# Cross-attention stack on one core: where TensorE's side steps stand between scores and outputs

## The reference, cut to what matters

```python
q = split_heads(x @ wq); k = split_heads(ctx @ wk); v = split_heads(ctx @ wv)
attn = softmax(q @ k.T * scale)      # 56 queries a head, 1500 keys (1496 in the third piece)
x = (attn @ v) joined @ wo + bo + x  # 20 heads of 64, 8 heads of 20, 20 heads of 8
```

## Time and profile before

| what | value |
|---|---|
| median of 3 runs | 5894.31 us (5889.82 to 5895.18) |
| the profiled execution, its own time | 5887.77 us |
| its span | 5886.0 us |
| TensorE busy (matmul) | 5530.6 us, 94% |
| TensorE weight loads | 4544.8 us, 77% |
| VectorE / ScalarE / GpSimd busy | 2818.9 / 3097.9 / 3117.4 us (48 / 53 / 53%) |
| mean granted clock of TensorE | 0.971 |
| chain that ended last, by engine | TensorE 62%, VectorE 20%, ScalarE 7%, GpSimd 3%, DMA 3%, issue 3% |

### The profile page before, as it was taken

One profiled execution on the slowest core, in us unless ns is written; L12 is line 12 of the kernel. 1 busy time (PEld: TensorE's weight loads), 2 busy tenths in 40 slices (PEclk: granted clock), 3 DMA queues, 4 the chain that ended last, 5 costly groups with the idle time before them and its releaser, 6 DMA issues.

```text
span 5886.0 us, 92283 instructions
## 1 busy us (share of the span) xinstructions
PE 5530.6 (94%) x34224; PEld 4544.8 (77%) x34224; DVE 2818.9 (48%) x5171; ACT 3097.9 (53%) x7280; POOL 3117.4 (53%) x3472
## 2 busy tenths in 40 slices
PE   7999999999999999998999999899999999999998
PEld 5777777778877777776767677578888888888887
DVE  2444454444444444443555555255454555445452
ACT  1455554555555555553555555265666565666655
POOL 0355554454444545553666666166666666566665
PEclk8899999999999999997999999599999999999998
DMA  2000000000000000000111111000000000000000
GB/s 57 13 17 14 17 17 17 17 17 13 14 13 17 17 17 17 14 22 17 31 30 30 32 28 43 11 20 19 17 21 17 21 20 21 17 18 20 17 21 12
DMA packets 85964, 119.97 MB, mean 20 GB/s; under 512 B 42814, under 2 KB 65194, under 8 KB 85514
## 3 DMA queue, kind: packets, MB, share of 16 engines
q1 hardware_dynamic: 85514, 114.07, 6.9%
HBM read 109.56 MB, written 4.46 MB: 19 GB/s over the span
## 4 chain that ended last, share of the span: by engine, by line
PE 62%; DVE 20%; ACT 7%; POOL 3%; DMA 3%; issue 3%; SPq 1%; ACTq 0%; POOLq 0%; DVEq 0%
PE ps_c L701 14%; DVE mpiece L1466 9%; PE ps_s L1141 5%; PE ps_s L1143 5%; PE ps_s L1142 5%; PE ps_c L1084 4%; PE ps_u L1156 4%; PE ps_u L1158 4%; PE ps_u L1157 4%; PE ps_c L1102 3%; POOL p_lo L1622 2%; DVE ctx_hi L1457 2%; DVE uT L1493 2%; ACT p_hi L1835 2%; ACT p L1833 2%
## 5 line engine op out<-in xcount | busy, mean ns | idle before, releaser
L1622 POOL TENSOR_TENSOR p_lo<-p,p_hi 125x448 fp32r<-125x448 f32 (+2 forms) x2688 | 2729.4, 1024 | 2215.3 <-ACT p_hi L1835 1623.4
L1833 ACT ACTIVATE p<-ps_s 125x448 f32<-125x448 f32 (+2 forms) x2688 | 1325.7, 493 | 1882.8 <-PE ps_s L1143 1668.7
L1835 ACT ACTIVATE p_hi<-ps_s 125x448 fp32r<-125x448 f32 (+2 forms) x2688 | 1316.9, 490 | 0.0
L1466 DVE TENSOR_REDUCE mpiece<-ps_c 125x1 f32<-125x500 f32 (+1 forms) x1984 | 1229.3, 668 | 86.0 <-PE ps_c L1084 80.4
L1141 PE MATMUL ps_s<-q_hi,ctxT_hi 105*125 105x448 f32 (+3 forms) x2688 | 999.1, 372 | 35.5 <-ACT p_hi L1835 29.1
L1156 PE MATMUL ps_u<-p_hi,ctx_hi 125*97 125x448 f32 (+2 forms) x2688 | 955.3, 355 | 1.5 <-POOL p_lo L1622 1.0
L1084 PE MATMUL ps_c<-ctxT_hi,q_hi 96*125 96x500 f32 (+1 forms) x2112 | 846.6, 425 | 104.6 <-DVE mpiece L1466 85.3
L1142 PE MATMUL ps_s<-q_lo,ctxT_hi 96*125 96x448 f32 (+2 forms) x2688 | 918.4, 342 | 0.0
L1143 PE MATMUL ps_s<-q_hi,ctxT_lo 96*125 96x448 f32 (+2 forms) x2688 | 916.6, 341 | 0.0
L1157 PE MATMUL ps_u<-p_hi,ctx_lo 125*96 125x448 f32 (+2 forms) x2688 | 909.5, 338 | 0.0
L1158 PE MATMUL ps_u<-p_lo,ctx_hi 125*97 125x448 f32 (+2 forms) x2688 | 909.0, 338 | 0.0
(11 more groups left out here) (228 smaller groups left out, 5861.6 us busy)
## 6 DMA issues: line engine op xcount, KB each, us to landing
ctx_raw<-in_ctx SPq DMA_DIRECT2D x96, 562.5 KB
pT<-recs SPq DMA_DIRECT2D x32, 490.0 KB, 3.6
w_area<-recs SPq DMA_DIRECT2D x32, 490.0 KB, 3.7
w_area<-recs SPq DMA_DIRECT2D x32, 196.0 KB, 3.8
cs<-in_ctx SPq DMA_DIRECT2D x192, 6.0 KB, 2.9
x_between<-x_out SPq DMA_DIRECT2D x32, 80.0 KB
x_in<-x_between SPq DMA_DIRECT2D x32, 80.0 KB
w_area<-in_L_xattn_wq SPq DMA_DIRECT2D x2, 800.0 KB, 5.9
```

The source lines that it names most:

```text
L1466: z = V.tensor_reduce(mpiece[0:wide, k, r:r + 1], C(0, wide, n % banks(t), 0, PIECE), AX.X, ALU.max)
L1622: P.tensor_tensor(p_lo[0:kp, k % 3, 0:w], p32[0:kp, k % 2, 0:w], p_hi[0:kp, k % RING, 0:w].bitcast(F32), ALU.subtract).then_inc(*sig("pl_r ...
L1833: A(p32[0:kp, k % 2, 0:w], ps_s[0:kp, k % 2, 0:w], ACT.Exp, scale=DH[t.ph] ** -0.5)
L1835: A(p_hi[0:kp, k % RING, 0:w], ps_s[0:kp, k % 2, 0:w], ACT.Exp, scale=DH[t.ph] ** -0.5)\
```

## The change

One line of TensorE's `main` goes:

```diff
@@ -1165,7 +1165,6 @@
                         pe.wait_ge(*got("ctx_lo", t, NLO * (b + 1)))
                     if n < total:
                         scores(n)
-                    yield 2 * n + 1
                     if n >= BEHIND or not first:
                         outputs(n - BEHIND)
```

## The result

The changed kernel takes 6053.18 us in the median of 4 runs (6049.38 to 6059.19), the kernel before 5894.75 us (5889.82 to 5896.51) in as many: a ratio of 1.0271, 95% interval 1.0253 to 1.0289. It is slower by 158 us. The forecast had the sign and a third of the size (50 us), and its range ended at 6005 us.

The account below looks back on a forecast made before the run. TensorE's own instruction stream plus its waits was taken to bound the kernel. Losses of 82 us (105 with `maxima` terms halved) less 30 us gains gave +52, said as +50: 5944 us, range 5866 to 6005 us.

Parts of the forecast that it names:

- `pre` 25 to 27: `pre` 25 feeds 27 through two VectorE passes; with 25 behind its outputs, 0.62 us more wait each: 9.3 us loss.
- `pre` 35 to 37: `pre` 35 feeds 37 through VectorE's copy with 0.15 us to spare; a wait of 0.47 us is left: 7 us loss.
- `pre` 2, 4, 16 and the step behind it: Cover gained at some of these steps and lost at others: `pre` 16 net 2 us loss, 2 and 4 taken as nothing.
- context, exponentials, scores: Phases 0 and 2: later context pieces delay ScalarE's copies, exponentials and the scores by 0.62 us, 30 times: 19 us loss.
- phase 1, `pre` 16: A later context piece makes ScalarE later with `xT`, for which `pre` 16 already waits: 15 x 0.65 = 10 us loss.
- outputs that wait themselves, and small ones: Phase 1's first outputs come earlier and wait for a copy, 6.5 us; other outputs and small losses, 5 us.
- gains at `pre` 8 and 34, and in phase 2: Outputs fill waits of `pre` 8 for VectorE and 34 for ScalarE, 9 us gain; a like phase 2 step, 3 us.
- `maxima`, losses halved, less their gains: Losses of 21, 15 and 10 us in phases 1, 2 and 0, halved; gains of 8 us in phase 1, 4 in phase 0.
- Four such places a pair: Phase 1 `maxima` on two banks: three matmuls in a row, the third waiting for VectorE's reductions: 21 us loss.
- counted at every matmul that has less to spare than it loses: Phase 2 `maxima` on three banks, VectorE reducing without pause: 9 us counted once a pair, 37 at every such matmul; 15 taken.
- The rival "much slower": Full `maxima` losses in phases 1 and 2, wider context delays, nothing relieved: +123 us, 6017 us; chance 0.18.
- The switch between kinds of work: 112 blocks of other work than `maxima` between scores and outputs each lose one TensorE switch: 6 us gain taken, 8 at most.

Follow-up runs that it names:

- short reductions: VectorE's maximum taken over only 125 of the 500 columns, in the kernel before and in the changed kernel: 5727.23 and 5773.31 us.
- the mirror of the change: Kernel before with side steps only between the scores and the outputs of a step, none ahead of the scores: 6012.76 us, ratio 1.0218.
- the fastest kernel: Kernel before with sixteen waiting side steps held back, plus a third place ahead of the outputs' last matmul for phase-0 `maxima` only: 5806.07 us, ratio 0.9859.

## Why the prediction was right in sign and wrong in size

Each term of the sum, against what the matched waits show in the changed kernel (us):

| term | forecast | measured |
|---|---|---|
| `pre` 25 to 27 | 9.3 | 8.6 |
| `pre` 35 to 37 | 7 | 6.6 |
| `pre` 2, 4, 16 and the step behind it | 2 | 3 (-3.9, +2.4, -4.1, +8.6 at `pre` 18) |
| context, exponentials, scores | 19 | 22.6 |
| phase 1, `pre` 16 | 10 | 9.8 |
| outputs that wait themselves, and small ones | 6.5 + 5 | 9.2 |
| gains at `pre` 8 and 34, and in phase 2 | -12 | -11.7 |
| not seen: `pre` 1 and context 3 in phase 1 | 0 | -19.9 |
| `maxima`, losses halved, less their gains | 23 - 12 = 11 | 110.4 |
| low clock | 0 | 29 |

**The chains were right.** The rows predicted one by one are there. Timeline of the changed kernel, the same steps of the same pairs as in the earlier trace rows:

```profile
1092.09 2.40 PEld L701 LDWEIGHTS ps_c<-w_area,hT 80*64 80x64 f32 x14 [1.11 <-DVE sm L1232]
...
1106.31 2.44 PE L907 MATMUL ps_c<-pT,kvb 128*128 128x64 f32 x20 [0.31 <-ACT pT L1707]
...
1113.81 0.29 PEld L913 LDWEIGHTS ps_c<-w_s,ones 1*128 1x128 f32 x2 [0.70 <-DVE qo L1331]
...
1619.73 0.18 PEld L1141 LDWEIGHTS ps_s<-q_hi,ctxT_hi 105*125 105x125 f32 x1 [0.81 <-ACT p_hi L1834]
...
3157.35 0.16 PEld L1156 LDWEIGHTS ps_u<-p_hi,ctx_hi 125*97 125x97 f32 x1 [0.93 <-issue]
...
3188.98 0.44 PEld L701 LDWEIGHTS ps_u<-xT,w_s 80*80 80x80 f32 x4 [1.19 <-ACT xT L1722]
```

Line 701 stands idle 1.11 us (1.1 forecast), line 913 0.70 (0.8), the scores behind the context pieces 0.81 where they had 0.19, which is the 0.62 of the outputs, and phase 1's `pre` 16 1.19 where it had 0.73. `pre` 34 waits 0.31 us less. The first outputs of a sequence in phase 1 now start late (row 3157.35); the view names no releaser there, but ScalarE's copy `uT` (line 1822) ends at 3157.24, just ahead.

**The step that failed is the term of the `maxima`:** 11 us net forecast, 110.4 measured. It failed in four places.
- "In phase 0 VectorE is the limit in most of each `maxima` stretch. There only the later start counts: 10 us." The later start did cost about that (8 us, seen where the `maxima` kept their places), but the whole came to 35.5. VectorE was not the limit without a break, as its wait for TensorE in phase 0 shows, before and after. And where it was the limit, its slower conversions (10.7 us more in phase 0) came on top, a term that the forecast did not have.

```profile
DVE mpiece L1466 <- PE ps_c L1084: 15.4, 42, 1.4
```

```profile
DVE mpiece L1465 <- PE ps_c L1084: 49.0, 80, 1.8
```

- "Four such places a pair, on average 0.35: 21 us." This is phase 1, and it came to 34.2, with the gains there already taken off.
- "counted at every matmul that has less to spare than it loses, 37. I take 15, nearer the low one, since after one wait the next ones are covered." This is phase 2. Measured 40.7. A wait does not cover the next ones: in the block it is followed by others, and VectorE catches up while scores and outputs run, so the next block begins from the same state.
- "The terms of `maxima` (21 + 15 + 10) fall where TensorE waits already, and a wait put ahead of these shortens them. I halve these terms". Nothing of the kind shows. The upper count of phase 2, 37, was nearly right, the 21 of phase 1 was too small even unhalved, and phase 0 should have had a count like that of phase 2. The gains that I set against them (8 and 4) are already in the measured sums.

The rival "much slower" named the mechanism in so many words, that joined matmuls leave VectorE idle while scores and outputs follow each other. What I held against it, that three banks hold 1.8 us of its work, is true only of three banks that are all unread. At 848.54 all three hold results, but VectorE is already in the first of them: 1.37 us of work are left, to 849.91, and the next result comes 1.66 us later, at 850.20. Even this rival ended at 6017 us, 36 below what was measured.

The signs that the prediction gave of itself told the same: it expected the wait of line 1084's loads to grow from 221 to some 240 us, most of it in phase 1, and it grew to 326.4, by 34, 30 and 42 us in phases 0, 1 and 2. VectorE's busy time, which should have stayed, grew by 47 us, 31 of them the conversions.

**What had no term at all is TensorE's clock**, the subject of the last section.

## What to carry to other kernels

Where a producer and a consumer exchange a few buffers, count the hand-overs by how they are grouped and not by their average rate: two places a step with one or two matmuls each kept VectorE better fed than one place with up to three, with the `maxima` moved alone, with short reductions and in the mirror of the change. And look at what else the engines do at that moment: an instruction of the consumer can grow from 0.34 to 1.25 us because it now starts behind one of a third engine. Price such a term at every hand-over that has less to spare than it loses, and don't halve it for waits that are there already. And a side step that waits is best held back by itself: a list of sixteen such steps, found in the trace, gave 68 us, while the rule that moved all of them at once lost 158.

## What the runs showed of the hardware that was not expected

**The clock falls more often in the changed kernel.** Three windows of 8 us in the changed kernel, phase 0: busy time of PE, PEld, DVE, ACT and POOL with instruction counts, granted clock, DMA share, GB/s.

```profile
640.00:648.00 8.00, 7.54 (x49) 6.19 (x47) 5.65 (x10) 4.77 (x14) 4.64 (x6) 1.00 0.01 2
648.00:656.00 8.00, 6.84 (x27) 5.31 (x26) 6.00 (x11) 2.42 (x7) 5.14 (x8) 0.79 0.05 12
656.00:664.00 8.00, 7.84 (x37) 5.55 (x35) 7.59 (x14) 3.64 (x10) 3.96 (x5) 1.00 0.23 75
```

TensorE's timeline in the middle one:

```profile
649.28 1.08 PE L1084 MATMUL ps_c<-ctxT_hi,q_hi 96*125 96x500 f32 x2 [1.06 <-DVE mpiece L1465]
650.20 0.37 PE L1141 MATMUL ps_s<-q_hi,ctxT_hi 105*125 105x448 f32 x1
650.41 0.37 PE L1142 MATMUL ps_s<-q_lo,ctxT_hi 96*125 96x448 f32 x1
...
650.84 0.55 PE L1156 MATMUL ps_u<-p_hi,ctx_hi 125*97 125x448 f32 x1
651.18 0.58 PE L1157 MATMUL ps_u<-p_hi,ctx_lo 125*96 125x448 f32 x1
651.56 0.58 PE L1158 MATMUL ps_u<-p_lo,ctx_hi 125*97 125x448 f32 x1
```

Directly after a wait of 1.06 us for VectorE the scores still stand 0.21 us apart. The outputs behind them stand 0.34 and 0.38 us apart where the earlier trace rows has 0.20: the engine has fallen to 1.2 GHz from 2.4, and a few steps later it is at 2.4 again. Such a stretch costs (1 - 0.79) x 8 = 1.7 us of full-speed time beside the wait itself. Summed in this way over all windows between the changes of phase, the kernel before has 5 stretches (8.5 us), the changed one 22 (37.2 us), with the `maxima` alone moved 30 (50.7 us), with the others alone 11 (18.5 us), the mirror 32 (82 us), the fastest kernel 1 (1.7 us). That is 29 us of the change's loss, and for the two halves of the change the clock alone comes to more than for the whole: (50.7 - 8.5) + (18.5 - 8.5) - 29 = 23 us more.

A wait of this length is not enough for a fall, and a fall does not need one. Shortly ahead of each of the 22 stretches TensorE stands idle for 0.9 us or longer. But between the changes of phase the changed kernel has 76 such waits, so most pass without a fall, and the kernel before has 51, with a fall behind one of them. The other four of its five stretches follow a block without a wait, 40 matmuls of 16 columns (line 778), as here in phase 2:

```profile
4535.11 2.30 PE L778 MATMUL ps_c<-vb_s,pT 128*64 128x16 f32 x40
...
4537.63 0.58 PE L1157 MATMUL ps_u<-p_hi,ctx_lo 125*96 125x448 f32 x1
4538.01 0.58 PE L1158 MATMUL ps_u<-p_lo,ctx_hi 125*97 125x448 f32 x1
```

The Trainium skill ("TensorE: Matmul & The Clock Gate", the section on a second failure mode) tells of a kernel whose frequent short idling between groups of matmuls makes the clock swing between its two levels; the changed kernel's trace agrees in so far as its 22 stretches follow idle time of 0.9 us or more. That the clock falls after these waits is read off the traces; no run removed the fall and kept the wait, so that the waits bring it about is not shown.

**A matmul behind one that has waited starts late.** Behind a `maxima` matmul that waited, the next matmul starts 0.33 us later (848.20 to 848.54); behind one that didn't, 0.23 us. That is 0.10 us beside each wait; some 90 more blocks end in such a pair, 9 us. It is not a net figure: over all `maxima` matmuls that scores or outputs follow, what starts later than 0.23 us adds up to 44 us in the trace of before and 41 in that of the changed kernel.

**The switch between kinds of work** costs about what was taken: the second matmul of wide scores or outputs comes 0.29 us after the first behind `pre`, `post` or context, and 0.21 behind a wide matmul. The changed kernel has 109 such blocks less, 9 us against the 6 that I took. The Trainium skill ("TensorE: Matmul & The Clock Gate", the part on what happens when a matmul is issued) says that weight loads are pulled ahead under conditions (no conflict of row groups, or a spare weight buffer). That a switch would then be free was my own step in the prediction, and the trace does not bear it out, with 0.29 against 0.21 us. Stalls 140, clock 29 and switches -9 make 160 us, with the late starts at 9 it is 169, against 161.6 between the two spans; the matching of the waits leaves a few us uncertain.
